# Layer 0 of a two-layer transformer kernel: VectorE's slot re-ordered, the rotation products merged, the transposition of keys and queries one slot later

## The reference, cut to what matters

```python
xn = layernorm(x)
qkv = xn @ w_qkv.T                         # 32 query heads, 8 key/value heads, head size 64
q, k = rms_norm(q, q_norm_w), rms_norm(k, k_norm_w)
q, k = q*cos + rot_half(q)*sin, k*cos + rot_half(k)*sin
scores = q k^T / 8, causal, window of 64   # four query heads share a key head
x = x + softmax(scores) v @ w_out.T + ffn(xn)
xn2 = layernorm(x)                         # and its product with the router's vector W_r
```

## Time and profile before

| | |
|---|---|
| median of 3 runs | 1046.46 us (1044.51 to 1050.87) |
| profiled execution | 1043.54 us, its span 1041.7 us |
| busy in the span: PE, DVE, ACT, POOL | 88%, 82%, 66%, 68% |
| granted clock, mean | 0.975 of full |
| layer 0 | from the start to about 668 us of the span |

### The profile page before, as it was taken

How to read it: one execution, slowest core, us unless ns; L and a number is a source line. 1 busy time by engine, 2 the same in 40 slices (tenths; PEclk the granted TensorE clock), 3 DMA queues, 4 the chain that set the end, 5 groups by cost and what they waited for, 6 DMA issues and landing times.

```text
span 1041.7 us, 26416 instructions
## 1 busy us (share of the span) xinstructions
PE 917.6 (88%) x8703; PEld 509.5 (49%) x8703; DVE 855.8 (82%) x1760; ACT 684.2 (66%) x1779; POOL 704.2 (68%) x1034
## 2 busy tenths in 40 slices
PE   3588898998998998998998997689999999999998
PEld 2355666665665765666665665342222222323223
DVE  6798778888888888788788786578999999899871
ACT  2555656655565665665565555127999999888885
POOL 3668878887888888888888878432766765444221
PEclk9799999999999999999999999879999999999999
DMA  5556644454444444444544444243221132222101
GB/s 195 128 115 131 106 96 78 96 99 82 90 98 82 90 99 81 92 98 83 96 97 82 86 90 91 44 134 65 60 43 23 23 41 42 52 43 46 28 1 42
DMA packets 247995, 82.57 MB, mean 79 GB/s; under 512 B 222196, under 2 KB 246452, under 8 KB 247604
## 3 DMA queue, kind: packets, MB, share of 16 engines
q1 hardware_dynamic: 247428, 78.53, 37.7%
q10 hardware_dynamic: 432, 2.36, 0.7%
HBM read 18.49 MB, written 4.19 MB: 22 GB/s over the span
## 4 chain that ended last, share of the span: by engine, by line
POOL 41%; issue 19%; DVE 18%; PE 17%; DMA 2%; SPq 1%; ACT 1%; POOLq 0%; DVEq 0%; ACTq 0%
DVE l_mxv L1333 17%; POOL rm L743 15%; POOL t L752 10%; POOL t L769 9%; PE l_mx L1535 6%; PE l_acc L1506 5%; POOL rs L743 2%; POOL tcw L788 1%; PE l_sc L1566 1%; POOL r L832 1%; PE l_sc L1543 1%; POOL r L830 1%; POOL xl L808 1%; DMA qkv_all<-w_qkv 1%; DMA ats<-an 1%
## 5 line engine op out<-in xcount | busy, mean ns | idle before, releaser
L1333 DVE TENSOR_REDUCE l_mxv<-l_mx 128x1 f32<-128x1024 f32 x256 | 295.1, 1215 | 26.9 <-PE l_mx L1535 26.2
L1246 ACT ACTIVATE l_prob<-l_sc 128x512 f32<-128x512 f32 x512 | 273.2, 604 | 18.0 <-PE l_sc L1543 16.7
L427 ACT ACTIVATE an<-an 128x256 f16<-128x256 f32 x128 | 53.3, 416 | 203.9 <-DVE an L601 203.8
L752 POOL TENSOR_TENSOR t<-t 128x320 f32<-128x320 f32 x128 | 110.5, 863 | 109.7 <-DVE t L648 109.6
L1535 PE MATMUL l_mx<-early 48*128 48x512 f16 x512 | 156.3, 387 | 20.3 <-DVE l_mxv L1333 14.3
L1543 PE MATMUL l_sc<-early 50*128 50x512 f16 x512 | 156.3, 383 | 0.3 <-ACT l_prob L1246 0.3
L743 POOL TENSOR_TENSOR rm<-ss,half_neg 128x5 f32<-128x5 f32 x128 | 156.5, 1223 | 0.0
L1506 PE MATMUL l_acc<-l_prob,qkv_all 128*17 128x256 f32 x2048 | 155.0, 387 | 0.0
L922 PE MATMUL ob<-wo_hi,ats 128*128 128x256 f16 x512 | 106.0, 275 | 33.6 <-DMA ats<-an 29.1
L880 PE MATMUL qk<-early,xh 128*128 128x384 f16 x512 | 130.2, 337 | 3.8 <-issue 3.4
L867 PE MATMUL pv<-v,probs 128*64 128x65 f32 x2048 | 89.0, 230 | 29.2 <-ACT probs L476 22.3
(11 more groups left out here) (187 smaller groups left out, 2058.7 us busy)
## 6 DMA issues: line engine op xcount, KB each, us to landing
qkv_all<-w_qkv SPq DMA_DIRECT2D x3, 768.0 KB, 9.1
v<-v SPq DMA_DIRECT2D x64, 32.5 KB, 2.0
xn_all<-xs SPq DMA_DIRECT2D x16, 128.5 KB, 2.1
xa<-x SPq DMA_DIRECT2D x16, 128.0 KB, 2.4
tk<-nat SPq DMA_TRANSPOSE x128, 2.8
qkv_all<-w_o SPq DMA_DIRECT2D x8, 256.0 KB, 3.7
ats<-an SPq DMA_TRANSPOSE x128, 2.5
xc<-x SPq DMA_DIRECT2D x16, 128.0 KB, 2.4
```

What stands on the lines that cost most here:

```text
L427: return act.activation(dst, src, ACT.Copy, scale=scale)
L752: pool.tensor_tensor(t1[:, b, :, :], t1[:, b, :, :], t2[:, :, :], ALU.add).then_inc(s_["pool_u"], 1)
L1246: act.activation(prob[:, (y * NI + u) % NPR, h * 512:(h + 1) * 512], sc[:, k % NSC, :], ACT.Exp, scale=D1 ** -0.5).then_inc(s_["act_sc"], 1)
L1333: dve.tensor_reduce(mxv[:, x % 2, u:u + 1], mx[:, MX[k] % 2, :], AX.X, ALU.max).then_inc(s_["dve_mx"], 1)
```

## The change: what it does

- DVE's slot begins with the key's low part, now of group s-6 (`LAG_K = 6`), then `xn`, the xs group and `xl`; then come V, output sum, feed-forward, O, A, the statistics, and the top-k. POOL's order stays as it was, and the slots in which each norm step is made stay the same too.
- L647 and L648 become one operation over 640 elements, with `qk` read twice: both products go into `tt` (two buffers). The swap of halves moves from DVE's read to POOL's read of the second product, and in the table from one factor to the other. `t2` had one buffer, so DVE waited for `pool_u` of the group before; now it waits for that of two before.
- SP issues the transposition of `nat` a slot later (LAG_K) and ahead of that of O. ACT's two copies move to lag 7: into `tk` as the first thing of its slot, out of `tk` where they were.
- Two waits on the shared tile `fa` are adapted to the new order.

```diff
+LAG_K = 6
-LAG_T = 6
+LAG_T = 7
...
-        t1 = sb("t1", [P, 2, NH, HD])
-        t2 = sb("t2", [P, NH, HD])
+        tt = sb("tt", [P, 2, 2, NH, HD])
+        t1 = tt[:, :, 0, :, :]
...
+                n, k, ok = at(s, LAG_T)
+                if ok:
+
+                    m = n * G + k
+                    wait(act, s_["pe_S"], m - NQ + 1)
+                    if m == 0:
+                        act.wait_ge(s_["set_k"], 1)
+                    ev(tk[:, m % NQ, 0:2, 0:WIN], kcs[:, n % B, k, :, :]).then_inc(s_["act_kc"], 1)
...
-                    dve.tensor_tensor(t1[:, b, :, :], heads, tcw[:, i % 2, 0, :, :], ALU.mult)
-                    dve.tensor_tensor(t2[:, :, :].rearrange("p h (a d) -> p h a d", a=2), swapped,
-                                      tcw[:, i % 2, 1, :, :].rearrange("p h (a d) -> p h a d", a=2),
-                                      ALU.mult).then_inc(s_["dve_A"], 1)
...
+                    wait(dve, s_["pool_u"], n * G + k - 1)
+                    dve.wait_ge(s_["act_A"], n * G + k + 1)
+                    dve.tensor_tensor(tt[:, b, :, :, :].rearrange("p j h d -> p j (h d)"),
+                                      qk[:, b, 0:NH * HD].unsqueeze(1).broadcast_to([P, 2, NH * HD]),
+                                      tcw[:, i % 2, :, :, :].rearrange("p j h d -> p j (h d)"), ALU.mult).then_inc(s_["dve_A"], 1)
...
-                    pool.tensor_tensor(t1[:, b, :, :], t1[:, b, :, :], t2[:, :, :], ALU.add).then_inc(s_["pool_u"], 1)
+                    pool.tensor_tensor(t1[:, b, :, :].rearrange("p h (a d) -> p h a d", a=2),
+                                       t1[:, b, :, :].rearrange("p h (a d) -> p h a d", a=2),
+                                       tt[:, b, 1, :, :].rearrange("p h (a d) -> p h a d", a=2)[:, :, ::-1, :],
+                                       ALU.add).then_inc(s_["pool_u"], 1)
```

More of the change, by code:

```diff
@@ L372, in _ @@
                     sp.dma_start(v0[WIN:P, n % B, k - 1:k + 1, :], v1[0:WIN, n % B, k - 1:k + 1, :]).then_inc(vnw[k // 2], 16)
[L373 to L381 removed]
+                n, k, ok = at(s, LAG_K)
                 if ok:
@@ L390, in _ @@
                                            ).then_inc(turned[m % NQ], 16)
+                n, k, ok = at(s, LAG_O)
+                if ok:
+                    m = n * G + k
+                    sp.wait_ge(s_["dve_al"], m + 1)
+                    wait(sp, s_["pe_W"], m - NA + 1)
+                    sp.dma_start_transpose(ats[:, m % NA, :, :, :].rearrange("p l a t -> p (l a) t"),
+                                           an16[:, m % 2, :, :, :].rearrange("p l i d -> p (l i d)")).then_inc(at_ld[m % NA], 16)
                 i = (s + 8) // 16
@@ L592, in _ @@
                 g = s % G
+                n, k, ok = at(s, LAG_K)
+                b = k % 2
+                if ok:
+                    dve.wait_ge(s_["act_kh"], n * G + k + 1)
+                    dve.tensor_tensor(nat[:, b, 1, 0:HD], t1[:, b, 0, :], nat[:, b, 0, 0:HD], ALU.subtract
+                                      ).then_inc(s_["dve_kl"], 1)
+                n = pair_tile(s + 1)
+                if n is not None:
+                    dve.wait_ge(s_["pool_rs1"], n + 1)
+                    wait(dve, s_["pe_lnt"], n)
+                    dve.tensor_scalar(xn[:, :], xa[:, n % B, :], mv1[:, n % B, 0:1], rs1[:, n % B, :],
+                                      ALU.subtract, ALU.mult).then_inc(s_["dve_xn"], 1)
@@ new lines, in _ @@
+                n = s // G - 2
+                if g == 3 and 0 <= n < NT:
+                    par = n % 2
+                    dve.wait_ge(s_["pool_rs2"], n + 1)
+                    dve.scalar_tensor_tensor(mv3[:, par, :], rs2[:, par, :], -LN_EPS, rs2[:, par, :], ALU.mult, ALU.mult
+                                             ).then_inc(s_["dve_b3"], 1)
+                    wait(dve, xs_st[par], n // 2 * 16)
+                    wait(dve, raw_ld[par], n // 2 * 16)
+                    dve.tensor_scalar(xs[:, par, 0:D], xc[:, par, :], mv2[:, par, 0:1], rs2[:, par, :],
+                                      ALU.subtract, ALU.mult).then_inc(s_["dve_xs"], 1)
+                    dve.wait_ge(s_["dve_b3"], n + 1)
+                    dve.tensor_scalar(ve3[:, par, :], mv3[:, par, :], 1.0 + LN_EPS, None, ALU.add).then_inc(s_["dve_v3"], 1)
+                    dve.wait_ge(s_["dve_xs"], n + 1)
+                    wait(dve, s_["dve_h"], min(NI * NF, (s - 1 - LAG_H) // 16 * NF + min(NF, (s - 1 - LAG_H) % 16 // 2 + 1)))
+                    if n == 0:
+                        dve.wait_ge(l1w_ld, 16 * 4)
+                    dve.tensor_tensor_reduce(out=fa[:, :, :].rearrange("p b t -> p (b t)"), in0=xs[:, par, 0:D], in1=wr[:, :], scale=1.0, scalar=0.0,
+                                             op0=ALU.mult, op1=ALU.add,
+                                             accum_out=xs[:, par, D:D + 1]).then_inc(s_["dve_wr"], 1)
@@ new lines, in _ @@
+                if g == 5 and 0 <= n < NT:
+                    par = n % 2
+                    dve.wait_ge(s_["pool_rs3"], n + 1)
+                    dve.wait_ge(s_["dve_wr"], n + 1)
+                    wait(dve, s_["pe_xat"], n)
+                    dve.scalar_tensor_tensor(xl1[:, :], xs[:, par, 0:D], rs3[:, par, :], lnw[:, :], ALU.mult, ALU.mult
+                                             ).then_inc(s_["dve_xa"], 1)
+                    if n == NT - 1:
+                        dve.wait_ge(s_["dve_xa"], NT)
+                        dve.tensor_tensor(xl1[:, :], xl1[:, :], lnb[:, :], ALU.add).then_inc(s_["pool_xa"], 1)
```

60 lines of the change are left out of this document (4 added, 56 removed).

## The result

| | |
|---|---|
| kernel after, median of 4 runs | 1142.57 us (1142.22 to 1143.36) |
| kernel before, median of 4 runs of the same session | 1046.56 us (1044.51 to 1050.87) |
| ratio | 1.091, 95% interval 1.087 to 1.094 |
| profiled execution | 1142.22 us, its span 1140.4 us |
| granted clock, mean | 0.936 of full |

The changed kernel is 9.1% slower, 96 us. The forecast was 1151, with a range of 1103 to 1189.

What follows compares the result with a forecast made beforehand. Layer 0 was taken to run on a ring of VectorE, ScalarE and PE, no engine full. Profiled 1043.5 us + 84 (stalls) - 5 (SyncE) + 26 (clock) = 1148.5, plus 2.9 to the median: 1151 us, range 1103 to 1189.

Steps and rivals of the forecast that it cites:

- VectorE asks for `rs` too early by 2.8 us: At VectorE's slot start: POOL's power, last in its slot, is ready 2.8 us late, so VectorE stands about 3 us.
- The xs group, 1.7 each: Slots r = 3 and 11: products to next rc grow from 6.93 to 8.6 us, 1.7 each, 15 counted.
- The second-layer step, 3.3 each where an L955 follows: Slots r = 5 and 13: 7.15 us become 10.4, 3.3 each in 13 tiles; two others at 1.7.
- xn, 1.7 at r = 1 and 0 at r = 15: Same wait for POOL: 1.7 us at r = 1, seven times; at r = 15 hidden behind PE's late V, taken as 0.
- The low part: Key's low part, moved first, is still held until POOL's addition ends; saving 0 to 5 us in all, taken as 0.
- SyncE: Transpositions: up to 23.1 us of PE's waits for O's could go, 5 taken; no new wait for `tk`.
- The clock, 26 us: PE idle behind stalls drops to 1.2 GHz, 0.7 or 1.7 us each, 39 us in all; two thirds taken, 26.
- the clock plays no part: Rival: PE has slack behind the stalls, so the low clock costs nothing; 1125 us, chance 0.17.
- PE's clock falls behind every stall: Rival: the low clock follows each stall, 39 us in place of 26, plus 12 in plain cases; 1176 us, chance 0.20.
- Absorbed: Rival: VectorE's 39.3 us of waiting for PE takes up part of the stalls, no clock term; 1086 us, chance 0.12.
- faster: Rival: low part clear of POOL's reads, 0.5 us shorter, and product 0.08, in 91 slots; 993 us, chance 0.04.
- nothing: Rival: gains and stalls cancel, so nothing to measure; 1046 us, chance 0.03.

Runs made afterwards that it cites:

- e1: The kernel before with xn, the xs group and the second-layer norm step alone moved first in VectorE's slot: 1163.46 us, 1.109 of before.
- e2: The changed kernel with all three norm steps put back at the end of VectorE's slot: 1038.33 us, 0.991 of before.
- e3: The changed kernel, norm steps still first, with POOL taking the powers rs1, rs2, rs3 first in its slot: 1044.27 us, 0.995 of before.
- e4: The changed kernel with 24 unused matmuls at the end of PE's slots r = 1, 3, 5, 11 and 13: 1148.57 us, 1.093 of before.
- e11: The changed kernel with all norm steps and the key's low part back at their old places: 1046.93 us, 0.997 of before.
- e8: The kernel before with the merged rotation product alone: 1050.54 us, 1.003 of before.
- e9: The changed kernel with the second-layer norm step back and 24 unused matmuls at the end of PE's slots r = 3 and 11: 1101.23 us, 1.047 of before.
- e6: The changed kernel with the xs group (r = 3 and 11) alone put back behind the slot's main work: 1127.85 us, 1.074 of before.

## Why the prediction was right

**VectorE asks for `rs` too early by 2.8 us.** Right, and the step that carried the case. The waits are 3.0 us in the mean (45.5 over 15, 44.8 over 15); e1 shows that this alone makes the loss, e2 and e3 that without it the loss is gone, from either side of the wait.

**The xs group, 1.7 each.** Measured by the pairs of slots: 1.9 and 1.8 us (11.1 against 9.2, 10.9 against 9.1). Right.

**The second-layer step, 3.3 each where an L955 follows.** The pairs grew by 3.6 and 3.5 us, which include 0.8 and 0.7 of low clock by e4; without it 2.8. The prediction had the clock as a term of its own, so the stall was put half a microsecond too high, and the pair comes out right by the two together.

**xn, 1.7 at r = 1 and 0 at r = 15.** Both too low: 2.3 and 0.9 came (11.64 against 9.37, 11.73 against 10.87). At r = 1 there was one thing more than the prediction had. The output sum (L657) stands in VectorE's queue behind xn, and PE's W of the next head group waits for it: 20.6 us over 7, against 1.4 before. That it is what makes the difference of 0.6 is likely and not shown. At r = 15 PE doesn't bring V late enough to hide 3 us of waiting.

**Together 11.7 in a round.** The round grew by 13.2 (90.3 less 77.1). In this are 1.5 of the low clock at r = 4 and 12, and a gain of 0.6 in the slots r = 6 to 9, nearly all of it the low part's (e11), 4 us in seven rounds: the prediction had "0 to 5" for it and took 0. Without these two the stalls are 13.2 - 1.5 + 0.6 = 12.3.

**The low part.** It still ends with POOL's addition: in the rows above it runs from 371.49 to 371.83, the addition to 371.75. It starts later against the addition, behind the statistics or the top-k step (0.61 us after the addition's start here, 0.42 in the earlier trace rows), and so is held for less: 381 ns against 707 in the median. It is the mechanism as written, and the saving was real rather than nothing. The rule of the Trainium skill on a VectorE instruction with two SBUF inputs beside a GpSimd instruction that reads SBUF (page "SBUF — State Buffer", section "Who interferes with whom") agrees with this row.

**The merged product, 0.80.** 0.82 measured; POOL's addition is unchanged at 0.86. e8 can't tell its effect on the time.

**SyncE.** PE's wait for O's transposition fell from 23.1 us to 5.0, as said. The other half was wrong: "no new wait" for `tk`, but PE's wait for it grew to 12.0 us from that of before,

```profile
PE sc L893 <- DMA tk<-nat: 1.9, 5, 0.7
```

and in e2, where the stalls are gone, to 23.1: the transposition of `nat`, issued a slot later, lands too late for PE in 25 slots. From 60 to 760 us PE's waits for the two transpositions sum to 28.5 us in e2 (5.4 and 23.1) and to 28.8 before (26.9 and 1.9): what the one gave, the other took.

**The clock, 26 us.** The term that was mis-sized, about 12 as measured: 9.6 at r = 4 and r = 12, and 2.3 at r = 13, where a low stretch fell in two of seven rounds (6.81 and 6.69 us against 5.58). Two steps of it failed. The prediction expected the low clock on PE's chain behind L955 (L962 in the changed kernel), at 1.7 us each for 13 tiles: in the seven rounds no low stretch reached r = 5 and two reached r = 13. And it priced the others by what one cost in the kernel before, and added that to the stalls; but a low clock that lies under the next step's stall costs only what reaches beyond it. The rival "the clock plays no part" (1125) was wrong by 12 us in this term and the forecast by 14, so neither had it. e9 shows the same clock at 22 to 28 us in a kernel with one stall fewer, and e6 shows the chain behind L955 at the low clock, 2.1 us longer, as the prediction feared.

**The 8 us by which 1151 is above the result.** 2.5 of them are the step from the profiled execution to the median, taken as 2.9 and measured as 0.4. The terms sum to 105 us of layer 0, and 96.5 came. Too much: 14 for the clock, 7 for the second-layer step (0.5 in 13 cases), 4 for the low part's saving that was taken as 0. Too little: 10 for xn (0.6 and 0.9 in seven rounds each), 2 for the xs group. That is 13 too much; the 5 us of SyncE's gain, which `tk` took back, bring it to 8. That the forecast is within 1% is in part luck: errors of 14, 10, 7 and 5 us stand against each other. (The rest of the span was 2 us longer than before.)

**The rivals.** "Absorbed" (1086), "faster" (993) and "nothing" (1046) fell with the result, and e1 to e3 show why. "PE's clock falls behind every stall" (1176) fell as well: 44 waits for `rs`, 23 low stretches. That VectorE's wait for PE could take up the stalls: it grew instead, from 39.3 us to 53.8.

Two things stay open: where the part of e2's 0.9% lies that is not the low part's, and why the stretch behind layer 0, with the same instructions, has the clock at 0.96 to 0.97 in some executions and at 0.94 in others.
